# Moving the first LayerNorm's normalisation of each batch from VectorE to ScalarE, and new slots for the score maxima

## The reference

```
x = x + 0.5 * ffn(layernorm(x))
x = x + attention(layernorm(x))
x = x + 0.5 * ffn(layernorm(x))
```

## Time and profile before

| | |
|---|---|
| median of 3 runs | 1042.67 us |
| the profiled execution's own time | 1045.78 us |
| its span, first to last instruction | 1044.0 us |
| mean granted TensorE clock | 0.926 |
| PE busy | 904.0 us, 87% |
| VectorE busy | 714.9 us, 68% |
| GpSimd busy | 745.7 us, 71% |
| ScalarE busy | 534.4 us, 51% |

### The profile page before, as it was taken

The page is one execution under the profiler, slowest core; times in us unless marked ns, Lnnn a source line. Parts: engine busy times, 40 slices in busy tenths (PEclk is TensorE's granted clock), DMA queues, the critical chain, the costliest instruction groups (busy, mean ns, idle before and its releaser), DMA issues. The chain is left out here.

```text
span 1044.0 us, 18096 instructions
## 1 busy us (share of the span) xinstructions
PE 904.0 (87%) x6174; PEld 545.9 (52%) x6174; DVE 714.9 (68%) x1526; ACT 534.4 (51%) x1065; POOL 745.7 (71%) x807
## 2 busy tenths in 40 slices
PE   4668889899898989899898989899898989998863
PEld 3345455556464656566465655555564656554323
DVE  4468577878777677868877777778777777675112
ACT  3243545556555555556555555556555646554530
POOL 4102669777786869777787868787777868786853
PEclk9868989999999999989998999999899999998875
DMA  3435341433434241523434240513334241400000
GB/s 78 103 73 131 72 94 29 108 75 72 110 70 111 50 103 31 118 64 72 110 72 110 61 119 21 118 47 88 94 72 110 62 110 39 113 12 21 1 21 10
DMA packets 77531, 77.66 MB, mean 74 GB/s; under 512 B 9392, under 2 KB 51136, under 8 KB 77440
## 3 DMA queue, kind: packets, MB, share of 16 engines
q1 hardware_dynamic: 75296, 74.76, 30.3%
q10 hardware_dynamic: 2144, 1.75, 0.7%
HBM read 9.90 MB, written 8.39 MB: 18 GB/s over the span
## 5 line engine op out<-in xcount | busy, mean ns | idle before, releaser
L417 POOL TENSOR_TENSOR first_probs<-first_probs,later_probs 128x768 f32<-128x768 f32 (+1 forms) x256 | 395.4, 1554 | 32.9 <-PE bank L644 32.9
L902 DVE TENSOR_REDUCE maxima<-bank 128x1 f32<-128x512 f32 (+1 forms) x384 | 258.5, 678 | 123.9 <-PE bank L693 123.1
L631 PE MATMUL bank<-q_stack,keys 123*128 123x512 f32 (+1 forms) x704 | 316.3, 479 | 20.1 <-ACT first_probs L510 18.0
L510 ACT ACTIVATE later_probs<-bank 128x384 f32<-128x384 f32 (+1 forms) x448 | 231.5, 536 | 192.8 <-PE bank L631 191.4
L693 PE MATMUL bank<-keys,q_stack 122*128 122x512 f32 (+3 forms) x1024 | 273.3, 348 | 15.8 <-DVE maxima L902 11.4
L693 PEld LDWEIGHTS bank<-keys,q_stack 122*128 122x128 f32 x1024 | 194.7, 203 | 130.7 <-DVE maxima L902 60.6
L447 POOL TENSOR_SCALAR_AFFINE_SELECT later_probs<-later_probs 128x512 f32<-128x512 f32 x192 | 122.9, 640 | 148.2 <-ACT later_probs L510 148.2
L510 ACT ACTIVATE first_probs<-bank 128x512 f32<-128x512 f32 x256 | 140.4, 593 | 105.5 <-PE bank L631 101.0
L902 DVE TENSOR_REDUCE block_max<-bank 128x4 f32<-128x512 f32 x256 | 174.8, 683 | 27.1 <-PE bank L693 26.4
L631 PEld LDWEIGHTS bank<-q_stack,keys 123*128 123x128 f32 x704 | 132.6, 200 | 101.2 <-ACT first_probs L510 49.4
L644 PE MATMUL bank<-later_probs,lat 128*32 128x384 f32 (+2 forms) x1536 | 126.8, 404 | 6.7 <-POOL later_probs L447 6.7
(11 more groups left out here) (113 smaller groups left out, 897.9 us busy)
## 6 DMA issues: line engine op xcount, KB each, us to landing
q_stack<-q_high SPq DMA_DIRECT2D x256, 128.0 KB, 2.4
q_stack<-q_low SPq DMA_DIRECT2D x128, 128.0 KB, 2.5
out_dram<-x SPq DMA_DIRECT2D x32, 256.0 KB, 2.4
x_in<-in_L_attn_x_bld_dram SPq DMA_DIRECT2D x16, 256.0 KB, 3.2
x_back<-out_dram SPq DMA_DIRECT2D x16, 256.0 KB, 3.0
keys<-keys_staged SPq DMA_DIRECT2D x15, 192.0 KB, 2.5
keys<-keys_staged SPq DMA_DIRECT2D x30, 96.0 KB, 2.3
lat<-lat_staged SPq DMA_DIRECT2D x16, 64.0 KB, 1.9
```

Source lines behind the costliest of these rows:

```text
L417: nc.gpsimd.tensor_tensor(total, total, later_probs[j - 1][:, heads], ALU.add).then_inc(added, 1)
L510: nc.scalar.activation(probs_of(s)[:, e:e + heads, 0:n], scores[u % 2][:, 0:heads * n].rearrange("p (e q) -> p e q", e=heads), ACT.Exp).th ...
L631: nc.tensor.matmul(scores[u % 2][:, 0:heads * n], keys[par][:, PLAIN_BLOCK[j], :], q_stack[par][:, first:first + heads, j * P:L], start=Tr ...
L902: nc.vector.tensor_reduce(out, seg, AX.X, ALU.max).then_inc(a_free, 1)
```

## The change

- VectorE's four L952 are gone. ScalarE normalises the four tiles of the next input, as `Identity` with a scale and a bias for each token, in step 15. The code allows one tile behind each of the step's four places for an exponential (`FIRST_TILES`).
- `first_rstd` on GpSimd has two more small instructions, `-mean` and its product with `f_rstd`, in a new tile `first_shift`. Its semaphore counts six a batch and not four.
- `A_AT` is new: steps and slots of the 41 units.
- `SCALE_AT` starts at step 5, not 4: the first of the four scalings of the output goes behind the causal mask of step 4.
- The other `normalise` calls are written through tables now, with the same tiles in the same places; `Y_READ` is written otherwise and has the same value.

```diff
-A_AT = [[], [1, 1, 2], [0, 2], [3, 5], [0, 2, 5], [0, 1, 1, 5], [0], [1], [3], [0, 1, 4, 5], [0, 1, 1, 2, 4], [4, 5, 5], [0, 2, 3], [0, 1, 4, 5], [0, 0, 2, 3], [5]]
+A_AT = [[], [0, 1, 1], [0, 2, 2, 3], [2], [3, 4], [0, 0, 1], [5], [1, 3], [1], [0, 1, 4, 5], [0, 0, 1, 2, 3], [5, 5], [0, 1, 3, 4], [1, 4, 5], [0, 2, 4], [1, 2, 3]]
...
-SCALE_AT = [4, 5, 5, 6]
+NORM_AT = [4, 10]
+NORM_TILES = [[0, 1], [2, 3], [], []]
+FIRST_TILES = [[0], [1], [2], [3]]
+SCALE_AT = [5, 5, 5, 6]
...
                 def first_rstd(off):
                     wait_batch_alone(pool, f_moments, t, off, 2, 1)
                     nc.gpsimd.tensor_scalar(f_var[:, 0], f_mv[:, 0, :, 1], EPS, None, ALU.add).then_inc(f_pool, 1)
-                    wait_batch(pool, f_pool, t, off, 4, 1)
-                    nc.gpsimd.tensor_tensor(f_rstd[:, 0], f_var[:, 0], neg_half[:], ALU.pow).then_inc(f_rstd_made, 1)
+                    nc.gpsimd.tensor_scalar(first_shift[:, 0], f_mv[:, 0, :, 0], -1.0, None, ALU.mult).then_inc(f_pool, 1)
+                    wait_batch(pool, f_pool, t, off, 6, 2)
+                    nc.gpsimd.tensor_tensor(f_rstd[:, 0], f_var[:, 0], neg_half[:], ALU.pow).then_inc(f_pool, 1)
+                    wait_batch(pool, f_pool, t, off, 6, 3)
+                    nc.gpsimd.tensor_tensor(first_shift[:, 1], first_shift[:, 0], f_rstd[:, 0], ALU.mult).then_inc(f_rstd_made, 1)
...
+                    for i in FIRST_TILES[e] if t + 3 < B and s == STEPS - 1 else []:
+                        if i == 0:
+                            wait_batch(act, f_rstd_made, t, 3, 2, 1)
+                            wait_batch(act, f_full, t, 2, F_UNITS, 3)
+                        last = nc.scalar.activation(xn[:, i, :], x_in[:, 1 - par, i, :], ACT.Identity,
+                                                    bias=first_shift[:, 1, i:i + 1], scale=f_rstd[:, 0, i:i + 1])
+                        if i == TT - 1:
+                            last.then_inc(f_normed, 1)
...
-                    if t + 3 < B and s == STEPS - 1:
-                        wait_batch(dve, f_rstd_made, t, 3, 2, 1)
-                        wait_batch(dve, f_full, t, 2, F_UNITS, 3)
-                        for i in range(TT):
-                            last = nc.vector.tensor_scalar(xn[:, i, :], x_in[:, 1 - par, i, :], f_mv[:, 0, i, 0:1],
-                                                           f_rstd[:, 0, i:i + 1], ALU.subtract, ALU.mult)
-                        last.then_inc(f_normed, 1)
```

More of the change, by code:

```diff
@@ L100 @@
 ADD_AT = [(1, 0, 2, 0), (1, 1, 2, 1), (2, 0, 3, 0), (2, 1, 3, 1)]
-SCALE_AT = [4, 5, 5, 6]
+NORM_AT = [4, 10]
+NORM_TILES = [[0, 1], [2, 3], [], []]
+FIRST_TILES = [[0], [1], [2], [3]]
+SCALE_AT = [5, 5, 5, 6]
 DEN_READ = (STEPS - 1 + max(lag for lags in WEIGH_ONES for lag in lags) + 1) % STEPS
-Y_READ = max(lag for lags in WEIGH for lag in lags)
+Y_READ = max(lag for r, lags in enumerate(WEIGH) for lag in lags if (r - lag) % TT == TT - 1)
 INVERT_AT = [2, 3]
@@ L517, in read_y, with normalise @@
                     nc.scalar.activation(y_sb[:, g, :], y_bank[:], ACT.Copy).then_inc(y_free, 1)
[L519 to L524, removed]
+                def normalise(s, e):
+                    for i in NORM_TILES[e] if prep and s == NORM_AT[0] else []:
+                        if i == 0:
+                            wait_batch(act, f_full, t, 2, F_UNITS, 1)
+                            wait_batch(act, f_rstd_made, t, 2, 2, 2)
+                        last = nc.scalar.activation(xn[:, i, :], x1[:, par, i, :], ACT.Identity,
+                                                    bias=f_shift[:, 1, i:i + 1], scale=f_rstd[:, 1, i:i + 1])
+                        if i == TT - 1:
+                            last.then_inc(f_normed, 1)
+                    for i in FIRST_TILES[e] if t + 3 < B and s == STEPS - 1 else []:
+                        if i == 0:
+                            wait_batch(act, f_rstd_made, t, 3, 2, 1)
+                            wait_batch(act, f_full, t, 2, F_UNITS, 3)
+                        last = nc.scalar.activation(xn[:, i, :], x_in[:, 1 - par, i, :], ACT.Identity,
+                                                    bias=first_shift[:, 1, i:i + 1], scale=f_rstd[:, 0, i:i + 1])
+                        if i == TT - 1:
+                            last.then_inc(f_normed, 1)
+                    for i in NORM_TILES[e] if end and s == NORM_AT[1] else []:
+                        if i == 0:
+                            wait_batch(act, t_rstd_made, t, -1, 1, 1)
+                        last = nc.scalar.activation(xn3[:, i, :], x2[:, i, :], ACT.Identity,
+                                                    bias=t_shift[:, 1, i:i + 1], scale=t_rstd[:, i:i + 1])
+                        if i == TT - 1:
+                            last.then_inc(t_normed, 1)
                 for s in range(STEPS):
@@ L548, in one_round @@
                         exp(s, 0)
[L549 to L555, removed]
+                    normalise(s, 0)
                     if s == DEN_READ and end:
@@ L561, in one_round @@
                         exp(s, 1)
[L562 to L565, removed]
+                    normalise(s, 1)
                     if attend:
                         exp(s, 2)
+                    normalise(s, 2)
                     if s == Y_READ - 1 and end:
```

4 lines of the change are left out of this document (3 added, 1 removed).

## The result

The changed kernel takes 992.67 us (median of 4 runs, 990.64 to 993.86), the kernel before beside it 1041.16 (4 runs, 1037.81 to 1043.9): the ratio is 0.9534, its 95% interval 0.9499 to 0.9569. The profiled execution took 992.4 us, 53.4 less than that of before; the medians differ by 48.5, so what follows from the two pages is some 5 us more than the kernels' usual difference. The forecast was 999 in a range of 981 to 1024.

What follows compares the result with a forecast made beforehand. The in-order PE stream sets a round's length. Saved per boundary: 2.34 + 1.42 - 0.2 = 3.56, x 13 = 46.3, less 2 at the start: 44.3 off the profiled 1045.78, 1001.5; median-adjusted 998.4, stated 999, range 981 to 1024.

Steps and rivals of the forecast that it cites:

- The wait for `xn`: At each round's boundary PE waits about 3.1 us for VectorE's normalised tiles; 2.34 us saved a boundary.
- The start: In round -2 ScalarE's tiles come ahead of the keys' DMAs, which leave later: 2 us lost, once.
- The delay of step 0 behind ScalarE's tiles: At the boundary the next step 0's exponentials, and the transposition of the maxima, come 0.79 us later.
- rival B: At the boundary ScalarE's tiles cost nothing, as step 15's three units may fill PE's time: 986 us, chance 0.15.
- GpSimd: Two added instructions make GpSimd's last additions at the boundary later; PE waits 0 to 0.6 us, 0.2 lost.
- rival C: At the boundary VectorE's reductions or GpSimd's additions replace `xn` as PE's wait, clock falling: 1035 to 1042 us, chance 0.05.
- The clock: PE's granted clock stays at 1.00, not 0.50, in the 3.41 us behind the boundary: 1.42 us saved a boundary.
- Rival A: At the boundary the wait goes but the clock behind it falls all the same: 1014 us, chance 0.2.
- New slots: Moved units of maxima, three in step 15 and two more in step 2: 0, within half a microsecond a round.
- `SCALE_AT`: The mask of step 4 goes before the first scaling, GpSimd's work up to the last scaling is unchanged: 0.
- Rival D: Crowded step 2 makes PE wait for reductions behind VectorE's inversions, clock falling: slower, 1061 us, chance 0.04.
- Why VectorE's tiles were slow: L952 takes 332 to 1371 ns because GpSimd, busy beside it at the boundary, contends for shared SBUF interfaces.

Runs made afterwards that it cites:

- e9: The changed kernel with two of ScalarE's four tiles of step 15 left out (half of `xn` isn't made): 992.32 us, ratio 0.9542.
- e10: e7 with two of ScalarE's four tiles of step 15 left out: 982.5 us, ratio 0.9412.
- e7: The changed kernel with `first_rstd` one step earlier on GpSimd: 979.97 us, ratio 0.9434.
- e1: The changed kernel with `A_AT` and `SCALE_AT` of before, so the move without the new slots: 997.9 us, ratio 0.958.
- e13: e1 with two of ScalarE's four tiles left out: 1000.55 us, ratio 0.9633.
- e6: The changed kernel with one more GpSimd `pow` in step 14, into a tile that nothing reads: 1006.55 us, ratio 0.9672.
- e4: The kernel before with three useless matmuls filling PE's wait for `xn` at each boundary: 1021.62 us, ratio 0.9801.
- e2: The kernel before with the new `A_AT` and `SCALE_AT` only, VectorE still normalising: 1061.84 us, ratio 1.0191.
- e3: The changed kernel with only `SCALE_AT` put back to 4, 5, 5, 6: 992.65 us, ratio 0.9524.
- e5: The kernel before with GpSimd's additions of a round's last head group cut to one column of each head: 981.39 us, ratio 0.9434.
- e12: The kernel before with `first_rstd` one step earlier on GpSimd and nothing else: 1038.39 us, ratio 0.9956.

## Why the prediction was right

The forecast lay 6.3 us above the measured time, and its mechanism is what the trace shows. Step by step:

- *The wait for `xn`.* Forecast: 2.34 a boundary, less 0.2 for GpSimd, times 13, less 2 at the start: 25.8 us of standing still. Measured: 25.4 from the two pages. That these agree so closely is luck, for the parts don't. The wait for `xn` itself fell by 42.2 - 2.1 = 40.1, all of it and not 2.34 x 13 = 30.4; the wait for GpSimd's additions grew by 22.8 - 4.8 = 18.0, and not by 2.6; the other waits together fell by 3.3. The start went better than forecast: the keys' DMAs are issued beside ScalarE's tiles, and the transposition of batch 1's input is at 46.01 in place of 47.25, so some 1.2 us gained where 2 were to be lost.
- *The delay of step 0 behind ScalarE's tiles*, forecast as 0.79, is the step that failed in this kernel. The stretch from the exponential of step 15 to the transposition of the maxima grew from 439.19 - 436.27 = 2.92 to 416.14 - 412.66 = 3.48, by 0.56, but e9 and e10 show that the tiles are no part of it: with two tiles it is 3.48 in e9 too. Two units more of maxima are in it now. This is rival B's mechanism; its 986 wasn't reached because of the next point, and e7, without that, is at 979.97. With the old slots the prediction's reason holds and only its size was off: e1 also has 3.48, e13 with two tiles less has 3.19.
- *GpSimd*, forecast as 0.2 a boundary out of 0 to 0.6, was mis-sized: 0.71 at the boundary. The additions end 418.99 - 412.66 = 6.33 behind the start of step 15's exponential, for 6.09 reckoned, and PE is ready for the sums 5.67 behind it, for 5.93 reckoned. It is where rival C looked, without the fall of the clock behind it. e6 and e7 price it: 13.9 us for a microsecond more, 12.7 back when the four small instructions are moved away. The waits for additions in other head groups, which come with the new slots, weren't in the prediction at all.
- *The clock*, forecast as 1.42 a boundary, was right for the boundary: e4's rounds give 1.4 to 1.7. In all it was too low, 18.5 for the 27.9 by which PE's busy time fell. The term counted only the 3.41 us behind the boundary. The falls behind step 4's wait in the earlier trace rows went too, six at some 0.6 each; and some 5 us of PE's busy time go with the new slots at the same clock. The factor of 0.42 was near enough: e4 has 58 us fewer at the half clock and takes 21.6 less, 0.37. Rival A, in which the clock falls all the same, is refuted.
- *New slots*, taken as 0 within half a microsecond a round: 5.2 us together with the move, 0.4 a round, inside that bound. Alone they cost 18.6 (e2); that the order in the stream makes a slot's price depend on L952 wasn't in the prediction. *`SCALE_AT`*: 0, as forecast (e3). Rival D's crowding of step 2 is a wait of 0.37 for a reduction at 425.03; all PE's waits for reductions of units together fell, from 11.7 us to 10.4.
- *Why VectorE's tiles were slow*: GpSimd beside them, shown by e5. The Trainium skill's page "GPSIMD Engine Reference" (Key points) names a sharing of SBUF interfaces between the two, and the runs agree: 665 against 341 ns. Whether VectorE's two-port mode, which it also names, is what is hit here, no run shows. The rule of "ScalarE: Activation LUTs" (Rules for kernel authors) that additions and multiplications belong on VectorE is overruled here by the measurement: the tile takes ScalarE 482 ns, more than VectorE alone (333), less than VectorE beside GpSimd (665).

Between the two profiled executions the gain was 53.4 for a forecast of 44.3: PE's busy time gave some 9 us more than forecast, and in the standing still the errors cancelled.

What stays open: where the new slots gain their 5.2 us. They don't gain them in waiting: PE stands still for 115.8 us in e1 and for 114.6 in the changed kernel. A round is 54.49 us with them and 54.75 with the old ones (intervals of the transposition of the input at the boundary), and most of that difference has come about by L743, in steps 13 and 14. From there to L730 both kernels take 4.98, though the new order has two units more in it; in e1 PE waits 0.44 in that place. This looks like work moved into a gap, but no experiment took those slots apart.

Open too is on what the fall of the clock behind step 4 depends. In the changed kernel the wait there is shorter, 0.80 in place of 1.18, and the clock falls in none of the 13 rounds. But in e1 the wait is 1.06 to 1.30, as long as before, and the clock falls in two rounds of 13 (they take 55.56 and 55.37), where before and e4 have six.

## What to carry to other kernels

Where one form of instruction, with the same data, is two or three times its minimum on VectorE, look at what GpSimd does beside it before calling the work expensive; an engine that is slower by itself can be the faster place for it. A PE stall can cost more than its length: here filling 13 waits of 3.1 us with useless matmuls made the kernel 21.6 us faster. When a wait is removed, ask which chain ends next, move small work out of that chain too, and expect that an edit worth little before the change (e12) is worth 12.7 us after it.

## What the runs showed of the hardware that was not expected

A copy of 128x8 elements on VectorE (L927) takes 167 ns in the median and at most 1214 beside GpSimd; at the boundary it took 1.04 us, longer than the reduction of 128x512 out of PSUM at 414.10, which took 0.68 with GpSimd busy beside it, no more than elsewhere. ScalarE's tiles of the same shape from SBUF lie between 477 and 494 ns in all 60 cases, whatever GpSimd does:

```profile
L540 ACT ACTIVATE xn<-x_in,first_shift,f_rstd x60: 477/482/494, 44.2 to 795.8; 128x128 f32<-128x128 f32 x60
```
```profile
L927 DVE COPY maxima<-block_max x32: 164/167/1214, 75.6 to 901.1; 128x8 f32<-128x8 f32 x32
```

And the granted clock of a stretch depends on more than the wait just ahead of it: behind step 4's wait of some 1.2 us it fell to 0.50 in six rounds of 13 before, in six with the boundary's wait filled (e4) and in two with the move alone (e1).
